# Graph layers on one Trainium2 core: softmax masks made in the logits, other node passes, no assertions, and a leak contraction in halves over four column strips

## The chip, the cores and the metric

The kernel runs on one core of one Trainium2 chip. The metric is device time in microseconds (us) of one execution. The core's engines are TensorE (PE in the profile; PEld is its weight load), VectorE (DVE), ScalarE (ACT), GpSimd (POOL) and SyncE (SP), which issues DMAs. ACT issues DMAs too, and so does POOL.

## What is computed

50000 nodes with 64 channels and 50000 edges, sorted by destination node `dst`. Four layers follow each other, and each one normalises x per node first (mean and variance over the 64 channels, then relu):

```python
h = relu(layernorm(x)); x = x + gated_conv(h, edges)      # layer 0
h = relu(layernorm(x)); x = x + edge_mlp_sum(h, edges)    # layer 1
h = relu(layernorm(x)); x = x + gatv2_twice(h, edges)     # layer 2, 5 heads, two rounds
h = relu(layernorm(x)); x = x + degree_conv(h, edges)     # layer 3, batch norm at the end

# one round of layer 2, with one self loop for each node
e = leaky_relu(xl[src] + xr[dst], 0.2)                    # 5 heads of 64 channels
alpha = einsum('ehc,hc->eh', e, att)                      # the logits
a = exp(alpha - segment_max(alpha, dst)[dst])
a = a / segment_sum(a, dst)[dst]
out = segment_sum(a * xl[src], dst).mean(heads) + bias
```

## The kernel before

The work is written out by hand for each engine, with semaphores; nothing is scheduled by a tool. `build` runs the stages one after the other, with a barrier between them (the class `Phase`). Nodes and edges are cut into 392 tiles of 128. `acc`, a buffer of 128 partitions x 27117 words, holds x or the sums.

`node_pass(layer)`, once ahead of each layer, goes over 28 groups of 14 tiles, four groups deep. DVE sums each node's channels (L595) and scales the sum to the mean (L599), POOL subtracts the mean from x (`centre`, L635), ACT squares the whole group (L660), DVE adds the squares up (L604), ACT takes the root (L665), DVE inverts it (L609) and makes h (L617, one instruction of two SBUF inputs and 896 elements). SP stores h twice, and in layer 2 x as well.

`attention_logits(g)`, for the two rounds g = 0 and 1, goes over 98 blocks of 512 edges. For each block POOL gathers the source rows by indirect DMA, and SP loads the rest. PE, in this order, transposes block n (`turn`), multiplies block n-1 by the weights (`project_whole`, L1531), takes the logits of block n-2 out of the leaky parts (`contract`) and does the last two products of block n-1 (`project_halves`, L1538). ACT makes the five leaky parts (L1572, L1577) and then issues the stores of the logits of block n-2 to `al_d` (L1563). DVE copies the transposed block (L1597), takes the logits out of PSUM (L1590) and makes the one-hot rows of a later block (L873). SP also stores the transposed block to `hsT_d` (L1491), out of a ring of two buffers: DVE's copy of block n waits for the store of block n-2.

`contract` writes one PSUM bank `alp` by strips: the output partitions fall into four strips of 32, and matmuls with 32 columns of weights on different strips run beside each other. The leaky parts q = 0, 1, 2 go to strips 0, 1, 2, the linear part (q = 5, in two matmuls of 256) goes to strip 3, and q = 4 and q = 3 are then added on strips 0 and 2. Every matmul of float32 stands in the trace as two instructions.

Ahead of its blocks each edge stage has a short loop, `fetch_rest` on POOL, `mask_rest` on DVE and `store_rest` on SP, and behind each edge stage stands `extra_pass`. Both treat the few edge tiles whose nodes lie outside the usual window, four in a turn and three turns in this run. Each turn reads four or eight tile numbers into registers, each with a check of its bounds at run time.

`softmax_stats(g)` lays the logits out as 125 rows (5 heads x 25 parts) of 2048 edges. SP loads 15 pieces of `dst_d` (own, previous and next destination) and 12 of `al_d`. DVE then makes masks out of the destinations, adds the two halves of each logit, and runs a segmented maximum and a segmented sum, each by a scan forwards and one backwards, an exchange of the rows' ends with PE, and both scans again with the carry (`both_ways`). At the end PE transposes the weights and DVE copies them out (L1755). POOL does nothing there.

## Time and profile before

| | us |
|---|---|
| median of 3 runs | 6159.76 (6159.35 to 6167.94) |
| the profiled execution | 6169.8, with a span of 6167.9 from the first instruction to the last |

| engine | busy, share of the span |
|---|---|
| PE | 4289.0 us, 70% |
| PEld | 2998.7 us, 49% |
| DVE | 3432.2 us, 56% |
| ACT | 3017.0 us, 49% |
| POOL | 3410.8 us, 55% |

The shares are averages over stages that follow each other and have different limits. So a change in one stage is read from that stage: from the rows of its timeline, and from the busy time in a window of it. Lines such as L1519 are lines of the kernel. What stands in brackets behind a row is the time for which the engine had been idle before it, and what ended that.

### The profile page before, as it was taken

The page shows a single profiled execution, that of the slowest core. Times are in us where ns is not written, and L with a number is a line of the kernel's source. Part 1 is how long each engine was busy: PE and PEld are TensorE (multiplying, and loading weights), DVE is VectorE, ACT ScalarE, POOL GpSimd, SP SyncE. Part 2 cuts the span into 40 slices and gives each one's busy share as a digit, 9 for nine tenths or more (in the row PEclk, how much of TensorE's full clock was granted, in tenths as well). Part 3 has the DMA queues.
Part 4 walks back from the last instruction along what each step waited for, and adds up shares of the span by engine and source line. Part 5 has one row for each costly group of instructions (what it writes and reads, how often), then busy time and mean ns, then how long its engine had stood idle before and what let it go on. Part 6 is the DMA issues. An engine that isn't in the chain of part 4 may idle for free. (4 is left out here: it accounts for less than half of the span.)

```text
span 6167.9 us, 123234 instructions
## 1 busy us (share of the span) xinstructions
PE 4289.0 (70%) x30675; PEld 2998.7 (49%) x30675; DVE 3432.2 (56%) x7378; ACT 3017.0 (49%) x6612; POOL 3410.8 (55%) x3519
## 2 busy tenths in 40 slices
PE   0089991499951999970995559999439877045564
PEld 0067771377740666640773236666237644035552
DVE  3834447677776222228888942222388688932256
ACT  0279992356631444430882224444138622755547
POOL 0866652566634544520886864454038699767720
PEclk9999995799975999985998989999769899567775
DMA  7566664565647444430333544444213333632224
GB/s 188 169 149 149 149 137 124 131 128 127 127 114 213 112 108 109 110 98 16 83 84 97 128 105 108 109 110 108 72 29 83 71 84 77 141 66 53 53 60 131
DMA packets 1392338, 664.98 MB, mean 108 GB/s; under 512 B 834785, under 2 KB 1339789, under 8 KB 1390450
## 3 DMA queue, kind: packets, MB, share of 16 engines
q1 hardware_dynamic: 1308640, 587.39, 38.1%
q0 software_dynamic: 64256, 65.93, 6.0%
q10 hardware_dynamic: 19320, 10.38, 0.7%
q14 instruction: 88, 0.72, 0.0%
q8 instruction: 34, 0.56, 0.0%
HBM read 393.69 MB, written 269.08 MB: 107 GB/s over the span
## 5 line engine op out<-in xcount | busy, mean ns | idle before, releaser
L849 POOL DMA_INDIRECT z_e<-h_d,src_i x784 | 770.3, 983 | 413.1 <-PE zTp_e L888 221.8
L1597 DVE COPY zT_l<-zTp_l 128x512 f32<-128x512 f32 x196 | 135.6, 692 | 1065.8 <-PE alp_l L1519 779.5
L1572 ACT ACTIVATE leak_l<-tp_l,bcat 128x512 f32<-128x512 f32 x588 | 403.7, 687 | 453.8 <-PE tp_l L1531 452.6
L734 ACT ACTIVATE hot_e<-iota_n,rel 128x256 f32<-128x256 f32 x1176 | 500.9, 501 | 232.3 <-PE part_e L747 226.3
L764 DVE TENSOR_TENSOR acc<-acc,part_e 128x128 f32 x1176 | 335.3, 285 | 472.1 <-PE part_e L747 343.0
L849 POOL DMA_INDIRECT z_l<-g_d,src_i x392 | 370.9, 946 | 350.0 <-PE zTp_l L888 255.4
L849 POOL DMA_INDIRECT z_l<-h_d,src_i x392 | 370.9, 946 | 349.9 <-PE zTp_l L888 254.9
L747 PE MATMUL part_e<-z_e,hot_e 128*128 128x128 f32 x1568 | 282.9, 355 | 383.1 <-DVE acc L1355 187.0
L1577 ACT ACTIVATE leak_l<-tp_l,bcat 128x256 f32<-128x256 f32 x784 | 307.7, 475 | 429.9 <-PE tp_l L1538 429.9
L884 PE MATMUL zTp_e<-ident,z_e 128*128 128x128 f32 x784 | 172.9, 303 | 468.7 <-DMA z_e<-rest_d 468.7
L747 PEld LDWEIGHTS part_e<-z_e,hot_e 128*128 128x128 f32 x1568 | 260.8, 260 | 405.3 <-DVE acc L1355 187.3
L734 ACT ACTIVATE hot_m<-iota_n,rel 128x256 f32<-128x256 f32 x784 | 334.3, 496 | 235.1 <-PEq L85 132.8
L1328 POOL DMA_INDIRECT z_e<-h_d,src_i x392 | 370.2, 944 | 139.9 <-issue 89.9
L635 POOL TENSOR_TENSOR xc<-acc,mean 128x896 f32<-128x896 f32 x112 | 189.0, 1688 | 453.4 <-DVE mean L599 453.0
L747 PEld LDWEIGHTS part_m<-m_m,hot_m 128*128 128x128 f32 x3136 | 365.4, 192 | 88.0 <-DVE acc L764 80.6
L747 PE MATMUL part_m<-m_m,hot_m 128*128 128x128 f32 x3136 | 402.6, 282 | 2.4 <-DVE acc L764 1.1
L747 PE MATMUL part_e<-m_e,hot_e 128*128 128x128 f32 x3136 | 386.4, 276 | 6.7 <-ACT hot_e L738 5.6
L747 PEld LDWEIGHTS part_e<-m_e,hot_e 128*128 128x128 f32 x3136 | 371.6, 192 | 16.1 <-issue 7.8
L1519 PE MATMUL alp_l<-leak_l,acat 128*32 128x512 f32 x1960 | 375.7, 600 | 3.3 <-ACT leak_l L1577 3.3
L1531 PE MATMUL tp_l<-zT_l,wcat 128*128 128x256 f32 x1176 | 371.2, 397 | 0.0
L1531 PE MATMUL tp_l<-zT_l,wswap_l 128*128 128x256 f32 x1176 | 350.2, 379 | 0.0
L884 PEld LDWEIGHTS zTp_e<-ident,z_e 128*128 128x128 f32 x784 | 79.0, 141 | 552.9 <-issue 541.3
(345 smaller groups left out, 11370.7 us busy)
## 6 DMA issues: line engine op xcount, KB each, us to landing
near_e<-near_d SPq DMA_DIRECT2D x784, 64.0 KB
near_l<-near_d SPq DMA_DIRECT2D x784, 64.0 KB
h_d<-h SPq DMA_DIRECT2D x84, 448.0 KB
near_d<-h SPq DMA_DIRECT2D x84, 448.0 KB
m_d<-m_m SPq DMA_DIRECT2D x196, 138.0 KB
relb_e<-rel_d SPq DMA_DIRECT2D x196, 128.0 KB
z_e<-rest_d SPq DMA_DIRECT2D x196, 128.0 KB
relb_l<-rel_d SPq DMA_DIRECT2D x196, 128.0 KB
```

Of the source, the lines that this page charges most:

```text
L635: nc.gpsimd.tensor_tensor(xc[g % DEEP][:, :, :], acc3[:, tiles(g), :], bc(mean[g % DEEP]), ALU.subtract).then_inc(n_cent, 1)
L734: ins = self.nc.scalar.activation(self.hots[k][:, t, :], self.S["iota_n"][:, :], ACT.Abs, scale=-1.0, bias=self.S["rel"][:, ds(n * BLK + t ...
L747: mm = self.nc.tensor.matmul(self.parts[t // 2][:, t % 2, w, :], self.hots[k][:, t, w * P:(w + 1) * P], m[:, t, :], start=True, stop=True)
L764: ins = self.nc.vector.tensor_tensor(x, x, part[:, t % 2, :, 0:x.shape[2]], ALU.add)
L849: self.nc.gpsimd.indirect_dma_start(out=self.z[n % RINGS][:, t, SIDES[t % 2]], out_offset=None, in_=self.table[:, :], in_offset=bass.Indir ...
L884: self.nc.tensor.matmul(zTp[:, t * P:(t + 1) * P], self.z[k][:, t, :], ident[:, :], start=(t == 0), stop=False, is_transpose=True, skip_gr ...
L1328: nc.gpsimd.indirect_dma_start(out=z[k][:, t, 0:C], out_offset=None, in_=S["h_d"][:, :], in_offset=bass.IndirectOffsetOnAxis(ap=S["src_i"] ...
L1519: mm = nc.tensor.matmul(alp[at:at + STRIP, :], acat[:, q, :], leak[k][:, q, :], start=(q in (0, 1, 2)), stop=(q not in (0, 2)))
L1531: mm = nc.tensor.matmul(by_side(tp[q])[:, side], left[:, q, :], by_side(zT[k])[:, side], start=True, stop=True)
L1572: nc.scalar.activation(leak[u % 2][:, q, :], tp[q][:, :], ACT.Relu, bias=bcat[:, 0, q:q + 1], scale=1.0 - SLOPE).then_inc(leak_ready, 1)
L1577: nc.scalar.activation(by_side(leak[u % 2][:, 3 + q, :])[:, side], tp[3 + side][:, q * 2 * P:(q + 1) * 2 * P].rearrange("p (r e) -> p r e" ...
L1597: nc.vector.tensor_copy(zT[k][:, :], zTp[k][:, :]).then_inc(zT_ready, 1)
```

## The change

1. **Logits, `contract`.** q = 4 is added on strips 0 and 1, one half of the block's 512 columns on each, and q = 3 on strips 2 and 3. A second weight tile `alate` gives q = 3 its place in strip 3. The logits of a block leave in six stores in place of four.
2. **Masks.** A class `Scan` owns the views of `acc` from ahead of the logits on. The 15 loads of `dst_d` are issued by ACT at the start of the logits. DVE makes the masks, and two new scans over them (`pf`, `pb`: is there no border between here and the row's end), between its first six blocks.
3. **Early loads.** Behind its last loads for the blocks, and ahead of the last three stores to `hsT_d`, SP issues 20 loads of the first 22 of 25 parts of each row. `softmax_stats` loads the other 3 parts by 20 small DMAs, ten on SP and ten on ACT.
4. **Softmax.** No reductions over the masks; in place of the second scans, one instruction each combines the held mask, the carry and the first scan. ACT takes over one mask and the copies of `als`, POOL takes over three operations on the self-loop side, and the division by 5 goes into another instruction.
5. **Node passes of layers 1 and 2.** The mean is subtracted on DVE, POOL does nothing, and ACT squares tile by tile, 14 instructions per group, each with the sum as its accumulator output. DVE's sum of the squares goes away.
6. **Assertions.** The loads of tile numbers in `mask_rest`, `store_rest` and `extra_pass` are made with no check of their bounds.

```diff
-STRIP_OF = (0, 1, 2, 2, 0, 3)
-STRIP_ORDER = (0, 1, 2, 5, 4, 3)
-STRIP_ROWS = ((0, 0, 4), (1, 4, 2), (2, 6, 4), (3, 10, 10))
+EARLY = 22
+AL_ROWS = ((0, 1, 4, 5, 6), (8, 9, 2, 3, 7))
+HALVES = (slice(0, BLK * P // 2), slice(BLK * P // 2, BLK * P))
+STRIP_ROWS = ((0, 0, 0, 2, ALL), (0, 2, 2, 2, HALVES[0]), (1, 0, 4, 2, ALL), (1, 2, 2, 2, HALVES[1]), (2, 0, 6, 4, ALL), (3, 0, 10, 10, ALL))
...
                 for g in range(G + 3):
                     if g < G:
                         add_up(g)
-                    if 2 <= g < G + 2:
+                    if 2 <= g < G + 2 and not SUMS_ON_ACT:
                         spread(g - 2)
+                    if g >= 3 and SUMS_ON_ACT:
+                        normalise(g - 3)
                     if g < G:
                         take_mean(g)
+                        if SUMS_ON_ACT:
+                            centre(g)
...
+                        for b in range(GRP):
+                            ins = nc.scalar.activation(sq[k][:, b, :], xc[k][:, b, :], ACT.Square, accum_out=var[k][:, b:b + 1])
+                        ins.then_inc(n_var, 1)
...
-                                                            min_val=0, max_val=TILES - 1)[1]
+                                                            min_val=0, max_val=TILES - 1,
+                                                                   skip_runtime_bounds_check_because="setup makes these numbers out of clamped tiles")[1]
...
+    def masks(self, dve, chain, step):
+        if step == 1:
+            dve.wait_ge(self.s_dst, 15 * 16)
+            chain(nc.vector.tensor_copy(self.tot, self.own.bitcast(I32)))
+            chain(nc.vector.tensor_copy(self.fwd, self.prev.bitcast(I32)))
+            chain(nc.vector.tensor_copy(self.bwd, self.nxt.bitcast(I32)))
+        if step == 2:
+            chain(nc.vector.tensor_tensor(self.prev, self.fwd, self.tot, ALU.is_equal))
+            chain(nc.vector.tensor_tensor(self.nxt, self.bwd, self.tot, ALU.is_equal))
+        if step == 3:
+            chain(nc.vector.tensor_scalar(self.pen_f, self.prev, 1.0, BIG, ALU.subtract, ALU.mult))
+            chain(nc.vector.tensor_scalar(self.pen_b, self.nxt, 1.0, BIG, ALU.subtract, ALU.mult))
+        if step == 4:
+            chain(nc.vector.tensor_tensor_scan(self.pf, self.prev, self.prev, 1.0, ALU.mult, ALU.min))
+        if step == 5:
+            chain(nc.vector.tensor_tensor_scan(self.pb[:, rev], self.nxt[:, rev], self.nxt[:, rev], 1.0, ALU.mult, ALU.min))
+            chain(nc.vector.tensor_scalar(self.own, self.pf, 1.0, BIG, ALU.subtract, ALU.mult))
...
+                def early():
+                    sp.wait_ge(scans.s_masked, 1)
+                    for k in range(2):
+                        sp.wait_ge(al_out[k], 96 * (EARLY * SCAN_W // (BLK * P) // 2))
+                    for part, pair in enumerate(((scans.lg, scans.ls), (scans.mx, scans.tot))):
+                        for side in range(2):
+                            scans.load_logits(sp, S["al_d"], pair[side], part, side, 0, EARLY, scans.s_early)
...
-                    for q in STRIP_ORDER:
-                        at = STRIP_OF[q] * STRIP
...
+                    for x, left, q, cols in ((0, acat[:, 4, :], 4, HALVES[0]), (1, acat[:, 4, :], 4, HALVES[1]),
+                                             (2, acat[:, 3, :], 3, HALVES[0]), (3, alate[:, :], 3, HALVES[1])):
+                        mm = nc.tensor.matmul(alp[strip(x), cols], left, leak[k][:, q, cols], start=False, stop=True, skip_group_check=True)
...
+                nc.gpsimd.tensor_tensor(ls, ls, tot, ALU.add).then_inc(self_sum, 1)
+
+                pool.wait_ge(s_a, 2)
+                nc.gpsimd.tensor_tensor(kept, prev, ls, ALU.mult).then_inc(self_kept, 1)
+                pool.wait_ge(self_kept, 1)
+                nc.gpsimd.tensor_tensor(kept, ls, kept, ALU.subtract).then_inc(self_kept, 1)
...
+                scans.load_logits(act, al_d, mx, 1, 0, EARLY, T, e_in)
+                scans.load_logits(act, al_d, tot, 1, 1, EARLY, T, x_in)
+                nc.scalar.activation(ppb, pb, ACT.Copy, scale=BIG, bias=-BIG).then_inc(s_pen, 1)
...
-                    chain(scan(fwd, gain_f, data, carry[:, 0:1], op0, op1))
-                    chain(scan(bwd[:, rev], gain_b[:, rev], data[:, rev], carry[:, 1:2], op0, op1))
+                    dve.wait_ge(s_pen, 1)
+                    chain(stt(out=fwd, in0=held_f, scalar=carry[:, 0:1], in1=fwd, op0=op0, op1=op1))
+                    chain(stt(out=bwd, in0=held_b, scalar=carry[:, 1:2], in1=bwd, op0=op0, op1=op1))
...
-                chain(ts(tot, tot, 1.0 / H, None, ALU.mult))
-                chain(tt(lg, lg, tot, ALU.mult))
-                chain(tt(ls, ls, tot, ALU.mult))
-                chain(ts(own, prev, -1.0, 1.0, ALU.mult, ALU.add))
-                chain(tt(ls, ls, own, ALU.mult))
+                chain(stt(out=lg, in0=lg, scalar=1.0 / H, in1=tot, op0=ALU.mult, op1=ALU.mult))
+                chain(stt(out=ls, in0=kept, scalar=1.0 / H, in1=tot, op0=ALU.mult, op1=ALU.mult))
```

On PE, the first `contract` of round 0, before (L1519 are the leaky parts, L1517 the linear one, L1538 the next product):

```order
L1519 MATMUL alp_l0<-leak_l0_0,acat0 32x512 x3
L1517 MATMUL alp_l0<-zT_l0_0,acat0 32x2x128
L1517 MATMUL alp_l0<-zT_l0_0,aswap_l0_0 32x2x128
L1519 MATMUL alp_l0<-leak_l0_0,acat0 32x512 x2
L1538 MATMUL tp_l0_3<-zT_l0_1,wcat0 128x256
```

and now:

```order
L1594 MATMUL alp_l0<-leak_l0_0,acat0 32x512 x3
L1596 MATMUL alp_l0<-zT_l0_0,acat0 32x2x128
L1596 MATMUL alp_l0<-zT_l0_0,aswap_l0_0 32x2x128
L1599 MATMUL alp_l0<-leak_l0_0,acat0 32x256 x3
L1599 MATMUL alp_l0<-leak_l0_0,alate_l0_0 32x256
```

The two matmuls of 512 columns at the end of the contraction have become four of 256.

On DVE, in the middle of the node pass of layer 1, before:

```order
564 L595 TENSOR_REDUCE mean_0<-acc 128x14
565 L604 TENSOR_REDUCE var_2<-sq_2 128x14
566 L599 TENSOR_SCALAR mean_0<-mean_0 128x14
567 L609 RECIPROCAL rstd_1<-rstd_1 128x14
568 L617 SCALAR_TENSOR_TENSOR h_1<-xc_1,rstd_1 128x896
```

and now:

```order
504 L599 TENSOR_REDUCE mean_0<-acc 128x14
505 L613 RECIPROCAL rstd_1<-rstd_1 128x14
506 L621 SCALAR_TENSOR_TENSOR h_1<-xc_1,rstd_1 128x896
507 L603 TENSOR_SCALAR mean_0<-mean_0 128x14
508 L627 TENSOR_TENSOR xc_0<-acc,mean_0 128x896
```

The sum of the squares has left DVE, and the subtraction of the mean has come to it.

On DVE, the first blocks of the logits of round 0, where the masks (the rows on `acc`) now stand:

```order
1224 L1681 COPY zT_l_0<-zTp_l_0 128x512
1225 L1499 CAST acc<-acc 125x2048
1226 L1500 CAST acc<-acc 125x2048
1227 L1501 CAST acc<-acc 125x2048
1228 L894 TENSOR_SCALAR hotT_l_0<-relb_l_2,iota_p 128x512 x2
1229 L1681 COPY zT_l_1<-zTp_l_1 128x512
1230 L1503 TENSOR_TENSOR acc<-acc 125x2048
1231 L1504 TENSOR_TENSOR acc<-acc 125x2048
1232 L894 TENSOR_SCALAR hotT_l_1<-relb_l_3,iota_p 128x512 x2
```

Before, the copy of a block was followed at once by the one-hot rows (L873) of the next.

## Rows read from the trace of the kernel before

**Rows 1.** Busy time by window: node passes of layers 1 and 2, then logits.

```profile
core 0: us, PE busy (x) PEld busy (x) DVE busy (x) ACT busy (x) POOL busy (x), PEclk, DMA share, GB/s
985.00:1090.00 105.00, 0.00 (x0) 0.00 (x0) 102.95 (x110) 27.43 (x45) 36.97 (x22) 0.50 0.66 192
1820.00:1920.00 100.00, 0.00 (x0) 0.00 (x0) 97.95 (x106) 26.39 (x42) 35.43 (x21) 0.50 0.91 288
...
2300.00:2400.00 100.00, 100.00 (x715) 60.52 (x705) 27.81 (x52) 47.42 (x92) 49.81 (x54) 1.00 0.46 110
```

**Rows 2.** Timeline (start, length, engine and line, operation): PE, a contraction and the next.

```profile
2307.03 0.63 PE L1519 MATMUL alp_l<-leak_l,acat 128*32 128x512 f32 x3
...
2307.92 1.03 PE L1519 MATMUL alp_l<-leak_l,acat 128*32 128x512 f32 x4
...
2308.88 0.48 PE L1538 MATMUL tp_l<-zT_l,wcat 64*128 64x256 f32 x1
...
2314.65 0.63 PE L1519 MATMUL alp_l<-leak_l,acat 128*32 128x512 f32 x3
```

**Rows 3.** Timeline: ACT's last stores of a block's logits, its next leak.

```profile
2311.15 1.20 ACTq L1563 DMA_DIRECT2D al_d<-logit_l  x3
...
2313.03 0.69 ACT L1572 ACTIVATE leak_l<-tp_l,bcat 128x512 f32<-128x512 f32 x1 [1.41 <-PE tp_l L1531]
```

**Rows 4.** Timeline: SP's loads of destinations at the softmax's start.

```profile
2742.42 5.94 SPq L1648 DMA_DIRECT2D acc<-dst_d  x15
```

**Rows 5.** DMA queues, packets, MB, share of 16 engines, from 2742 to 2800 us.

```profile
q1 hardware_dynamic: 1050, 7.17, 35.7%
```

**Rows 6.** Timeline: DVE in the softmax of both rounds.

```profile
2790.52 2.29 DVE L1691 TENSOR_TENSOR acc<-acc 125x2048 f32<-125x2048 f32 x1 [51.70 <-DMA acc<-al_d]
...
2795.17 1.23 DVE L1694 CAST acc<-acc 125x2048 f32<-125x2048 int32 x1
...
2847.18 2.29 DVE L1705 TENSOR_REDUCE flag_s<-acc 125x1 f32<-125x2048 f32 x1 [3.83 <-ACT acc L1683]
...
2866.10 4.48 DVE L1728 TENSOR_TENSOR_SCAN acc<-acc,carry_s 125x2048 f32<-125x2048 f32 x1
...
2909.24 3.52 DVE L1755 COPY als<-pt_s 128x125 f32<-128x125 f32 x16
...
4438.37 2.29 DVE L1691 TENSOR_TENSOR acc<-acc 125x2048 f32<-125x2048 f32 x1 [57.71 <-DMA acc<-al_d]
```

**Rows 7.** Timeline: POOL and DVE in layer 1's node pass, and after POOL's last.

```profile
1008.76 1.69 POOL L635 TENSOR_TENSOR xc<-acc,mean 128x896 f32<-128x896 f32 x1 [3.10 <-DVE mean L599]
...
1008.93 2.47 DVE L617 SCALAR_TENSOR_TENSOR h<-xc,rstd 128x896 f32<-128x896 f32 x1
...
1011.32 1.07 DVE L595 TENSOR_REDUCE mean<-acc 128x14 f32<-128x896 f32 x1
1012.32 1.07 DVE L604 TENSOR_REDUCE var<-sq 128x14 f32<-128x896 f32 x1
...
1013.71 2.46 DVE L617 SCALAR_TENSOR_TENSOR h<-xc,rstd 128x896 f32<-128x896 f32 x1
...
1098.74 1.09 DVE L617 SCALAR_TENSOR_TENSOR h<-xc,rstd 128x896 f32<-128x896 f32 x1
```

**Rows 8.** Timeline: ACT's small instructions in layer 3, and its accumulator reads.

```profile
5301.31 3.43 ACT L673 ACTIVATE hd<-h,dsc 128x64 f32<-128x64 f32 x14
...
6035.09 0.19 ACT L2270 ACTIVATION_READ_ACCUMULATOR y_f<-acc,col_f 128x1 f32 x1
6035.18 0.71 ACT L2270 ACTIVATE y_f<-acc,col_f 128x512 f32<-128x512 f32 x1
```

**Rows 9.** Timeline: DVE's idle time behind loads of tile numbers.

```profile
926.20 0.72 DVE L764 TENSOR_TENSOR acc<-acc,part_e 128x128 f32 x2 [0.33 <-issue]
...
957.59 0.63 DVE L1430 TENSOR_TENSOR at_r<-dstf,extra_lo 128x1 f32 x4 [3.66 <-issue]
...
1970.76 0.15 DVE L817 COPY left_l<-dst_i 128x1 int32 x1 [2.12 <-issue]
```

180 lines of the change are left out of this document (112 added, 68 removed).

## The prediction

> **What bounds the kernel now.** No engine bounds the whole: the stages do, each by something else. I read the busy time by window first, to find what is full in each stage that the change touches, and then the timeline there. The profiled execution took 6169.8 us (span 6167.9), 10 us over the median of the runs; the sum is made against the former and then lowered by 10.
>
> In the logits PE is busy for the whole of the window, at full clock, while DVE is busy for 28%, ACT for 47%, POOL for 50% and DMA for 46% [rows 1]. From one contraction to the next are 2314.65 - 2307.03 = 7.62 us, of which the contraction holds 1.85: 0.89 to the start of its last group, 0.96 from there to the next product [rows 2]. So what PE saves per block is saved 98 times in each round.
>
> In the softmax only DVE works, and first it stands idle for 51.7 us in round 0 and 57.7 in round 1 until its inputs have come [rows 6].
>
> In the node passes of layers 1 and 2 DVE is busy for 98% [rows 1]. A group takes 1013.71 - 1008.93 = 4.78 us, and of that 2.47 go to an instruction that takes 1.09 once POOL has stopped [rows 7]: DVE waits there for POOL's subtraction, which started 0.17 earlier. In layer 2 DMA is at 0.91 too.
>
> **Contraction in halves.** The first round of strips stays. In the last group two strips take 512 columns each, and now four take 256. The first group shows four strips side by side in 0.89 us for 512 columns each, so I take it that four halves too run side by side: 0.43 us instead of 0.86. Gain 0.43 x 98 x 2 = **84 us**. What is late next? POOL needs 5.0 us of the new 7.19 per block, DVE 2.1, so neither. ACT issues six stores instead of four, at 0.40 each; they end at 2312.35 now and the next leak starts at 2313.03 [rows 3], so they end about at the same point as that start, and PE reads this leak only in the next block but one. Bounds of this term: 0 (two halves follow each other) to 90.
>
> **Masks and loads in the logits.** DVE gets three casts, two comparisons, two masks, two scans and one more mask in five pieces, 3.7 to 5.7 us each from 1.23 for a one-input operation, 2.29 for two inputs and 4.48 for a scan [rows 6]. In a block of 7.2 us it has 5.1 free, and PE needs the copy of a block about 2 us after it can be made. Only the first piece stands where the blocks still ramp up; I charge 3 us. ACT's 15 loads are 3 MB, issued at 0.40 each [rows 4] while the short loop gathers rows; 7.17 MB took 48.1 us in the softmax [rows 5, 6], so 3 MB take 20, beside three turns of about 10 us. They cost the small gathers some latency: 4 us (0 to 12). For two rounds **+14 us**.
>
> **Early loads.** 20 x 22 x 8 KB = 3.6 MB, at that rate 24 us. They go into SP's queue right behind the store of block 94. The store of block 95 is queued behind them, and DVE's copy of block 97 waits for it: three blocks, 21.5 us, later. So it comes some 5 us late, PE waits for that copy and may take up its last block at a lower clock. I charge **8 us** a round (0 to 15). What is gained is DVE's wait: from the last logit (2790.52 - 51.70 = 2738.8) to SP's first load at 2742.4 [rows 4, 6] stay 3.6 us, and then ten small loads on each of two queues need about 4 us to issue and 2 to land. So DVE starts 10 us after the last logit in place of 51.7 and 57.7: 41.7 + 47.7.
>
> **Softmax chain**, per round, by DVE instructions that go [rows 6]: one addition and the masks 2.3 + 3 x 1.25 + 2 x 2.3 + 2 x 1.25 = 13.2; four reductions 9.2; four scans of 4.5 become one pass each of two inputs, 2.3, which is 8.8; of the 3.83 us of waiting for both exponentials 0.2 stay, 3.6; at the end two one-input passes and one two-input pass, 4.8; of the 3.5 for the copies of als, ACT's run beside the others and 0.5 stays, 3.0. Sum 42.6. Against it stand POOL's three passes. Scaled from 1.69 for 896 elements [rows 7] each takes 3.9 us for 2048, and DVE's two-input instruction in rows 7 waited for the whole of POOL's. If all three are waited for, they cost 11.6; if the second and third fall beside the 5 us exchange with PE, less; no row shows a scan against POOL. I take 8 (0 to 11.6), near the upper end because of rows 7. Net 34.6.
>
> The Trainium skill (SBUF — State Buffer, Who interferes with whom) says that a DVE instruction with two SBUF inputs contends with a GpSimd instruction that reads SBUF, and that the loser fully blocks. The trace agrees for L617. By that rule alone the charge would be 11.6 and the sum 7 us smaller; by a cost that only POOL bears it would be 16 larger.
>
> Softmax in all: 41.7 + 47.7 - 2 x 8 + 2 x 34.6 = **143 us**.
>
> **Node passes.** DVE's group becomes a sum, a reciprocal, h in 1.09, the mean, and the subtraction, about 1.09 as well: some 3.7 us. ACT's becomes 14 squares with accumulator and a root. Fourteen instructions of 64 elements with a scale from memory started 0.24 apart (3.43 less the last one's end, over 13), and a read of the accumulator puts 0.09 between its start and the next instruction's [rows 8]: 14 x 0.33 + 0.2 = 4.8 us, no gain. The square has no scale from memory and should be cheaper, with 0.17 at the lowest: 3.9. I take 4.1, since the squares are plain. Layer 1 gains 0.7 x 28 = 19. In layer 2 DMA at 0.91 lets 4.78 fall to 4.4 at most [rows 1]: 8. Together **27 us** (from a loss of 5 to 37).
>
> **Assertions.** DVE is idle for 3.66 us behind two checked loads and 2.12 behind one, so a checked load costs up to 1.54; an unchecked one, 0.33 or less [rows 9]. So a check costs some 1.2. In `extra_pass` both of DVE's loads lie on the path of each turn: 5 passes x 3 turns x 2.4 = 36. In the short loops one: 4 x 3 x 1.2 = 14. **50 us** (25 to 65). SP's loads run beside DVE's.
>
> **Sum.** 84 + 143 - 14 + 27 + 50 = 290 us. 6169.8 - 290 = 5880, and 10 less for the median: **5870 us**.
>
> **Rivals.**
> 1. The halves do not run side by side: the sums on strips 0 and 1 read the same weights and the same leaky part. If two follow two, the last group keeps 0.86, and the 84 us are gone: 5954. If all four follow each other it takes 1.72 and PE gets slower by 168: 6122. Against it: the first group's four strips, two of which read the same buffer too.
> 2. ACT bounds the node passes. If a square takes its whole 0.33 us and the read its whole 0.19, a group takes 14 x 0.52 + 0.3 = 7.6 us, 2.8 over now, 157 us for both passes: 5870 + 184 = 6054. Against it: the rows show both overlapped.
> 3. The wait moves: the small loads queue behind each other or behind the early ones, and half of the 89 us of DVE's wait stay: 5915.
> 4. Slower than before: the six stores per block. ACT's own work is 47% of 7.62, 3.6 us per block, and if its sequencer issues a store only between computations, a block takes 3.6 + 6s. That exceeds PE's 7.19 from s = 0.6 on, and eats up all other gains (206 us, 1.05 per block over 7.62) from s = 0.85. At s = 1.0 a block takes 9.6 us: 5964 + 1.98 x 196 = 6352. The rows have s = 0.40, beside running computations.
> 5. The change does less than it says: were only the contraction and the early start to work, with chain, node passes and assertions without effect, 84 + 89 - 30 = 143 us would remain: 6017.
>
> **How the numbers follow.** The forecast with its small variations has 0.66, by itself 5810 to 5930; rival 1 0.10 (mostly its milder form), rival 2 0.08, rival 3 0.09, rival 4 0.02, rival 5 0.05. Below the forecast stand: no stall at the logits' end (16), no wait for POOL (16), node passes and assertions at their ends (10 and 15), dst loads for nothing (8). The range 5800 to 5960 takes these in, rival 3 and the milder rival 1, and leaves out the rest, some 0.18. A measurement of this kernel can tell about 0.2% (12 us) from no change. Faster: all but rival 4 and a residue, 0.96; the same 0.01; slower 0.03.
>
> **What would show it.** Right: contractions 7.2 us apart, with 0.5 us in the last group; DVE's first instruction of the softmax some 10 us after the last logit, and copies of al ending 85 to 90 us later; groups of 4.1 us in layer 1 and 4.4 in layer 2; idle time of 1.3 us at the start of a turn of `extra_pass`. Wrong: a wait of PE for a leak in the middle of the logits; more than 10 us of PE idle ahead of its last block; accumulator reads 0.5 us apart; DVE instructions of 2048 elements lengthened by more than 12 us in all, beside POOL.

## The result, and the profile after

The changed kernel takes 5905.49 us in the median of four runs (5902.51 to 5907.38), beside 6160.15 us for the kernel before in the same session: a ratio of 0.958, with a 95% interval of 0.9568 to 0.9593. The forecast was 5870 us, the range 5800 to 5960. The profiled execution took 5907.4 us with a span of 5905.6, so between the two traces lie 262 us; the forecast had 290.

**Contraction.** Timeline of PE in the logits of the first round (start, length, engine and line, operation, count), against [rows 2]:

```profile
2625.26 0.63 PE L1594 MATMUL alp_l<-leak_l,acat 128*32 128x512 f32 x3
...
2626.14 0.39 PE L1599 MATMUL alp_l<-leak_l,acat 128*32 128x256 f32 x3
...
2626.69 0.48 PE L1618 MATMUL tp_l<-zT_l,wcat 64*128 64x256 f32 x1
...
2632.46 0.63 PE L1594 MATMUL alp_l<-leak_l,acat 128*32 128x512 f32 x3
```

The next contraction follows after 7.20 us, not 7.62, and the last group holds 0.55 us, not 0.96. The forecast said 7.2 and 0.5.

**Far rows.** Ahead of the blocks, three turns gather 12 tiles of far rows. DVE waits for a gather in each of four masks of a turn. Here are its timeline in the first and second turn and, in the DMA view from 1898 to 1938 us (bytes of a tile, then median us from issue to landing), what was in flight:

```profile
1907.61 0.26 DVE L845 TENSOR_SCALAR hotT_l<-hotT_l,far_l 128x64 f32<-128x64 f32 x1 [6.93 <-DMA hotT_l<-h_d,left_l]
...
1912.17 0.15 DVE L838 COPY left_l<-dst_i 128x1 int32 x1 [1.03 <-issue]
...
1920.51 0.25 DVE L845 TENSOR_SCALAR hotT_l<-hotT_l,far_l 128x64 f32<-128x64 f32 x1 [7.39 <-DMA hotT_l<-h_d,left_l]
1924.09 0.26 DVE L845 TENSOR_SCALAR hotT_l<-hotT_l,far_l 128x64 f32<-128x64 f32 x1 [3.33 <-DMA hotT_l<-h_d,left_l]
```

```profile
q10 hardware_dynamic: 450, 3.07, 20.0%
q1 hardware_dynamic: 1904, 0.71, 7.8%
q0 software_dynamic: 412, 0.43, 5.0%
...
acc<-dst_d ACTq DMA_DIRECT2D x15, 200.0 KB
...
hotT_l<-h_d,left_l POOLq DMA_INDIRECT x12, 5.5
```

The second turn starts 1.03 us behind the first one's end, where it was 2.16: the assertion is gone. But the gathers come late. The new 3.07 MB lie on ACT's queue (q10) beside them. From the first turn's start to the last mask the trace before has 28.02 us in round 0 and 27.67 in round 1, the trace after 37.84 and 39.71. For the kernel before, the same waits read:

```profile
1954.38 0.25 DVE L824 TENSOR_SCALAR hotT_l<-hotT_l,far_l 128x64 f32<-128x64 f32 x1 [2.73 <-DMA hotT_l<-h_d,left_l]
1955.80 0.27 DVE L824 TENSOR_SCALAR hotT_l<-hotT_l,far_l 128x64 f32<-128x64 f32 x1 [1.17 <-DMA hotT_l<-h_d,left_l]
```

Turn by turn round 0 takes 12.4, 17.5 and 8.0 us, where it took 10.0, 10.1 and 7.9. In the first turn only the landing of the gathers is late. In the second POOL also asks for them late: it gathers into the buffers out of which SP stores the first turn's rows to `rest_d`, and waits for these stores. Here are POOL's first operation of the second turn (a small addition ahead of its first gather), now and before, and the DMA view from 1907 to 1912 us, with the four stores of the first turn:

```profile
1914.81 0.19 POOL L829 TENSOR_TENSOR spare_l<-iota_p 128x1 f32<-128x1 f32 x1 [8.79 <-DMA rest_d<-hotT_l]
```

```profile
1961.14 0.19 POOL L808 TENSOR_TENSOR spare_l<-iota_p 128x1 f32<-128x1 f32 x1 [4.34 <-DVE far_l L818]
```

```profile
rest_d<-hotT_l SPq DMA_DIRECT2D x4, 32.0 KB, 8.9
```

The stores of the kernel before's first turn land after 1.5 us.

**The logits' end and the start of the softmax.** Timelines of SP's queue, DVE and POOL, against [rows 6]:

```profile
2629.42 7.77 SPq L1491 DMA_DIRECT2D acc<-al_d  x20
...
2637.23 1.21 SPq L1560 DMA_DIRECT2D hsT_d<-zT_l  x2
```

```profile
2677.14 2.29 DVE L1793 TENSOR_TENSOR acc<-acc 125x2048 f32<-125x2048 f32 x1 [10.85 <-DMA acc<-al_d]
2679.46 4.42 DVE L1798 TENSOR_TENSOR_SCAN acc<-acc 125x2048 f32<-125x2048 f32 x1
2683.92 8.53 DVE L1799 TENSOR_TENSOR_SCAN acc<-acc 125x2048 f32<-125x2048 f32 x1
...
2726.85 2.47 DVE L1808 TENSOR_TENSOR_SCAN acc<-row_s 1x125 f32<-1x125 f32 x1
```

```profile
2681.22 6.95 POOL L1765 TENSOR_TENSOR acc<-acc 125x2048 f32<-125x2048 f32 x1 [60.90 <-DMA acc<-al_d]
2713.70 6.78 POOL L1768 TENSOR_TENSOR acc<-acc 125x2048 f32<-125x2048 f32 x1 [25.53 <-ACT acc L1780]
2720.56 8.49 POOL L1770 TENSOR_TENSOR acc<-acc 125x2048 f32<-125x2048 f32 x1
```

DVE starts 10.85 us after the last logit (forecast 10) where it was 51.70. DVE copies block 95 by 2634.8, SP issues its store at 2637.23, behind the 20 loads, and it lands behind their 3.6 MB, 17.6 us later. Block 97's copy waits for that landing:

```profile
2654.79 0.69 DVE L1681 COPY zT_l<-zTp_l 128x512 f32<-128x512 f32 x1 [12.06 <-DMA hsT_d<-zT_l]
```

PE waits for that copy, and takes up its last block with products of 1.22 us, where the same two took 0.70 in the block before; its granted clock is 0.50 (1.2 GHz) from 2655 to 2658 us, behind 6.12 us in which it did nothing, and was 1.00 (2.4 GHz) from 2640 to 2648:

```profile
2655.54 1.22 PE L1611 MATMUL tp_l<-zT_l,wcat 128*128 128x256 f32 x2 [6.12 <-DVE zT_l L1681]
```

Beside POOL the reverse scan takes 8.53 us, not 4.42. POOL's first operation starts at 2681.22, inside the forward scan that ends at 2683.88, and ends at 2688.17: 4.29 us after the scan's end. The reverse scan, issued at 2683.92, ends at 2692.45, which is 4.28 us after POOL's end. Both figures are near the 4.42 us of the undisturbed scan and the 3.9 that I had expected of POOL, so I read them as each engine's own work, none of it beside the other's. DVE copies al by 2765.0, 87.9 us after its first operation.

**Node pass of layer 1 and turns of an extra pass.** DVE, against [rows 7] and [rows 9], then the busy time by window in the passes of layers 1 and 2, against [rows 1]:

```profile
1004.09 1.08 DVE L599 TENSOR_REDUCE mean<-acc 128x14 f32<-128x896 f32 x1
1005.09 0.23 DVE L613 RECIPROCAL rstd<-rstd 128x14 f32<-128x14 f32 x1
1005.42 1.09 DVE L621 SCALAR_TENSOR_TENSOR h<-xc,rstd 128x896 f32<-128x896 f32 x1
...
1006.64 1.09 DVE L627 TENSOR_TENSOR xc<-acc,mean 128x896 f32<-128x896 f32 x1
1007.64 1.08 DVE L599 TENSOR_REDUCE mean<-acc 128x14 f32<-128x896 f32 x1
```

```profile
949.43 0.63 DVE L1454 TENSOR_TENSOR at_r<-dstf,extra_lo 128x1 f32 x4 [1.44 <-issue]
```

```profile
core 0: us, PE busy (x) PEld busy (x) DVE busy (x) ACT busy (x) POOL busy (x), PEclk, DMA share, GB/s
1000.00:1060.00 60.00, 0.00 (x0) 0.00 (x0) 57.64 (x86) 60.00 (x494) 0.00 (x0) 0.50 0.89 259
1800.00:1860.00 60.00, 0.00 (x0) 0.00 (x0) 46.83 (x70) 50.91 (x410) 0.00 (x0) 0.50 1.00 303
```

A group of layer 1 takes 3.55 us (forecast 4.1, before 4.78). In layer 2 the first twelve groups take 3.55 too; from then on DVE waits for stores of h out of the ring, most groups take 4.4 to 4.7, and the DMA share is 1.00.

**Where the 262 us are.** Each number is a time in the traces from DVE's first instruction of a stage to its first of the next. In the logits that is now the fill of the new weight tile, 1.7 us ahead of the first turn; from the first turn on, the logits take 1534.4 us, 41.7 less, and the pass ahead of them is then 4.6 shorter, not 6.3.

| stage | before | after | less |
|---|---|---|---|
| edges of layer 0 (with the wait ahead of its extra pass) | 659.8 | 651.5 | 8.3 |
| node pass, layer 1 | 141.2 | 113.8 | 27.4 |
| edges of layer 1 | 665.2 | 660.8 | 4.4 |
| node pass, layer 2, up to the logits | 147.0 | 140.7 | 6.3 |
| logits to the last logit, both rounds | 1576.2 | 1537.8 | 38.4 |
| last logit to the first softmax operation, both | 109.4 | 21.9 | 87.5 |
| softmax, both | 251.8 | 187.6 | 64.2 |
| five extra passes | 121.0 | 99.8 | 21.2 |
| all else | | | 4.6 |

### The profile page after: what moved, and what is told of

The parts are those of the page before. It is cut to its first block and busy times, and to the rows that moved or that the text cites. A ratio compares the mean times of both kernels' runs of the same rounds, so it can differ in the third digit from the quotient of the medians.

```text
span 5905.6 us, 126888 instructions
## 1 busy us (share of the span) xinstructions
PE 4208.6 (71%) x31459; PEld 3024.1 (51%) x31459; DVE 3357.9 (57%) x7332; ACT 3145.2 (53%) x8158; POOL 3384.5 (57%) x3469
## 5 line engine op out<-in xcount | busy, mean ns | idle before, releaser
L1681 DVE COPY zT_l<-zTp_l 128x512 f32<-128x512 f32 x196 | 135.5, 691 | 959.5 <-PE alp_l L1599 692.8
L870 POOL DMA_INDIRECT z_l<-h_d,src_i x392 | 384.6, 981 | 300.1 <-PE zTp_l L909 203.5
L870 POOL DMA_INDIRECT z_l<-g_d,src_i x392 | 384.8, 982 | 299.2 <-PE zTp_l L909 202.3
L767 PEld LDWEIGHTS part_m<-m_m,hot_m 128*128 128x128 f32 x3136 | 365.2, 192 | 87.9 <-DVE acc L784 80.6
L905 PE MATMUL zTp_l<-ident,z_l 128*128 128x128 f32 x784 | 173.6, 304 | 251.7 <-DMA z_l<-rest_d 248.3
L2175 DVE TENSOR_TENSOR prod_a<-xl_a,wself_a 128x640 f32<-128x640 f32 x392 | 303.8, 814 | 56.1 <-PE xl_a L2062 56.0
```

What stands on the lines that cost most here:

```text
L767: mm = self.nc.tensor.matmul(self.parts[t // 2][:, t % 2, w, :], self.hots[k][:, t, w * P:(w + 1) * P], m[:, t, :], start=True, stop=True)
L870: self.nc.gpsimd.indirect_dma_start(out=self.z[n % RINGS][:, t, SIDES[t % 2]], out_offset=None, in_=self.table[:, :], in_offset=bass.Indir ...
L905: self.nc.tensor.matmul(zTp[:, t * P:(t + 1) * P], self.z[k][:, t, :], ident[:, :], start=(t == 0), stop=False, is_transpose=True, skip_gr ...
L1681: nc.vector.tensor_copy(zT[k][:, :], zTp[k][:, :]).then_inc(zT_ready, 1)
L2175: nc.vector.tensor_tensor(prod[k][:, 2 * q:2 * q + 2, :].rearrange("p t (h c) -> p t h c", h=H), xl[slot(u, q)][:, :, 0:HC].rearrange("p t ...
```

## Experiments

Runs of one group ran on one chip. In groups one and two the kernel before took 6497.7 and 6500.0 us, in group three 6166.2. Where the groups differ is told at the end; a run is compared with the changed kernel on its own kind of chip (groups one and two were two chips of one kind), and small effects are read from the length of their stage, since a ratio's interval is some 8 us to either side.

### Group one

**The contraction alone**, in the kernel before:

```diff
-                    for q in STRIP_ORDER:
...
+                    for x, left, q, cols in ((0, acat[:, 4, :], 4, HALVES[0]), (1, acat[:, 4, :], 4, HALVES[1]),
+                                             (2, acat[:, 3, :], 3, HALVES[0]), (3, alate[:, :], 3, HALVES[1])):
...
-                    for strip, at, rows in STRIP_ROWS:
+                    for strip, row, at, rows, cols in STRIP_ROWS:
```

> The kernel before with only the contraction of the change: the fourth and fifth leak in halves over the four column strips, the extra left-hand tile, and six stores of logits a block instead of four. Theory: the contraction is the bound of the logits in both rounds, its period goes from 7.62 to 7.19 us and nothing else moves, so 196 blocks save 84 us: 6160 becomes about 6076 us, and each round's logits take 746 instead of 788 us from the first mask turn to the last logit. Rival: the two more stores a block on ScalarE's queue or their landing hold the logit tiles back and eat half of it; each round's logits would take 767 us and the kernel 6118 us.

Measured: 6441.4 us, ratio 0.9914 (0.9899 to 0.9929), 56 us less, 46 to 66 by the interval. The gain lies between the theory's 84 and the rival's 42. The logits take 770.3 and 769.0 us from the first turn to the last logit, near the rival's 767, but not for the rival's reason: on this chip the first logit comes 32 to 34 us after DVE's first comparison for the blocks (the first of `hotT`), where the kernel before has 21 to 22 on the first chip. In the blocks of round 0 PE's recorded waits sum to 4 us, most of them for ACT's leaky parts; the changed kernel on the first chip has 0.2 us of them. Median distance of two logits: 7.24 and 7.26 us. From the first logit to the last are 704.4 and 701.1 us, against 732.9 in both rounds of the kernel before on the first chip. So the halves do run beside each other, and no wait of DVE for the stores of the logits stands among its waits; but of 84 us this run shows at most 66. There is no trace of the kernel before on this chip, so the whole gain is only known here from the times.

**Loads of node numbers late**, in the changed kernel:

```diff
+                act.wait_ge(z_used, 1)
                 scans.load_nodes(act, S["dst_d"])
...
-                        scans.masks(dve, chain, n)
+                        scans.masks(dve, chain, n - 3)
```

> The changed kernel with the 15 loads of node numbers issued on ScalarE's queue only when TensorE has used the first block of rows, and the five mask steps on VectorE three blocks later (ten blocks of the logits are written out ahead of the loop, not six). Theory: in the changed kernel these loads run beside the three turns that gather the far rows and lengthen them from 28.0 to 37.8 us a round, though a turn has lost its assertion; moved behind, the turns take about 25.5 us, the logits of each round are 12 us shorter, and the kernel goes from 5905 to about 5881 us. Rival: the loads take the same DMA time from the first blocks' row loads instead, TensorE waits there as long, and the kernel stays at 5905 us. Second rival: the turns are long for another reason (their own gathers or the code), and stay at 37.8 us.

Measured: 6285.0 us; the changed kernel takes 6275.9 on such a chip (group two). The turns take 25.83 and 25.72 us, as the theory said; so the loads had lengthened them. But the first logit comes 48.7 and 50.5 us behind DVE's first comparison, where the changed kernel has 32.3 and 31.6 on such a chip, and the stage up to the softmax's first operation is 0 and 8 us longer. DVE's timeline shows for what it waits there:

```profile
2194.94 0.88 DVE L894 TENSOR_SCALAR hotT_l<-relb_l,iota_p 128x512 f32<-128x512 bf16 x2 [17.66 <-DMA relb_l<-rel_d]
2206.60 0.69 DVE L1682 COPY zT_l<-zTp_l 128x512 f32<-128x512 f32 x1 [10.78 <-DMA hsT_d<-zT_l]
```

The first rival is right: the wait went to the next in line for the DMA engines.

**One store first**, in the changed kernel:

```diff
-    if between is not None:
-        between()
     for n in range(NB - lag, NB):
         then(n, n)
+        if n == NB - lag and between is not None:
+            between()
```

> The changed kernel with the 20 early loads of logits issued behind the first of the last three stores of rows, not ahead of it. Theory: VectorE's 12.06 us idle at the last but one block is the wait for that one store, which lies on SyncE's queue behind 20 loads; it goes, the last logit comes 6 us earlier in each round, and the early loads still land before the late ones: 5905 becomes about 5893 us, with VectorE's first softmax operation still 11 us behind the last logit. Rival: the early loads land so much later that softmax waits for them: the 6 us come back there (17 us behind the last logit) and the kernel stays at 5905 us.

Measured: 6265.7 us, 10 less than the changed kernel in group two. The last five logits come 7.10, 7.30, 7.09, 5.08 and 7.42 us apart, 34.0 us in all; in the changed kernel on such a chip it is 7.09, 7.31, 13.37, 7.42 and 4.21, 39.4. The stall at block 97 has gone, and part of it came back at the last one, where DVE now waits for stores of logits:

```profile
2915.82 0.75 DVE L1674 TENSOR_SCALAR logit_l<-alp_l,lin_b 128x512 f32<-128x512 f32 x1 [6.67 <-DMA al_d<-logit_l]
2927.70 2.29 DVE L1793 TENSOR_TENSOR acc<-acc 125x2048 f32<-125x2048 f32 x1 [11.13 <-DMA acc<-al_d]
```

Softmax starts 11.1 us behind the last logit, as before. The order in SP's queue was the larger half of the stall; the 3.6 MB in flight are the rest.

**GpSimd's three operations on VectorE**, in the changed kernel:

```diff
-            @block.gpsimd
-            def _(pool):
...
+                chain(tt(ls, ls, tot, ALU.add))
...
+                chain(tt(kept, prev, ls, ALU.mult))
+                chain(tt(kept, ls, kept, ALU.subtract))
```

> The changed kernel with GpSimd's three operations of the softmax (the sum of the two self logits and two for the kept part, each 125x2048) given to VectorE. Theory: in the changed kernel GpSimd working beside VectorE lengthens two reverse scans from 4.42 to 8.53 us and one scan of the row from 0.41 to 2.47 us, 10.3 us a round; on VectorE the three cost 3 x 2.3 = 6.9 us, so each chain gets 3.4 us shorter, 90 becomes 86.7 us, and the kernel goes from 5905 to about 5899 us. Rival: the scans are long for what they read or write now, not for GpSimd: they stay at 8.53 us, the three operations come on top, and the kernel goes to 5919 us.

Measured: 6265.6 us, 10 less. The softmax takes 90.43 us in the first round and 90.40 in the second, against 93.77 and 93.78 in the first trace of the changed kernel and 93.35 and 93.76 in its second: 2.9 to 3.4 less, where the theory had 3.4. The scans are short again:

```profile
2930.93 4.42 DVE L1787 TENSOR_TENSOR_SCAN acc<-acc 125x2048 f32<-125x2048 f32 x1
2935.39 4.42 DVE L1788 TENSOR_TENSOR_SCAN acc<-acc 125x2048 f32<-125x2048 f32 x1
```

So 6 to 7 of the 10 us are shown to be of this edit; the rest is within what the times vary.

### Group two

**The changed kernel again**, unedited:

> The changed kernel once more, so that the next three have it on their own chip. Theory and rival alike: ratio to the kernel before of 0.958 where the edge stages take what they took in the first pair of traces, nearer to 0.964 on a chip where those take longer; the three turns that gather the far rows take 37.8 us in the logits of the first round.

Measured: 6275.9 us, ratio 0.9655 (0.9642 to 0.9668). Turns 38.44 and 37.36 us, first logit 32.3 and 31.6 us behind DVE's first comparison, 719.1 and 717.1 us from the first logit to the last (first chip 700.4 and 702.1).

**Loads of node numbers spread**, three for each of five blocks:

```diff
+                def loads(n, u, i):
+                    body(n, u, i)
+                    if isinstance(n, int) and 2 <= n < 7:
+                        scans.load_nodes(act, S["dst_d"], n - 2)
...
-                        scans.masks(dve, chain, n)
+                        scans.masks(dve, chain, n - 7)
```

> The changed kernel with the 15 loads of node numbers issued by ScalarE three at a time behind its work on blocks 2 to 6, and the mask steps on VectorE at blocks 8 to 12 (14 blocks written out ahead of the loop). Theory: the loads cost time only where all 3 MB of them lie on the DMA engines at once, first beside the gathers' turns (37.8 us instead of 25.8), then beside the first blocks; three a block fit into what the steady blocks leave free, so the turns take 25.8 us, the first logit comes no later than in the changed kernel behind the turns, and each round gains 12 us: 24 us less than the changed kernel on this chip. Rival: the 3 MB cost their 12 us wherever they are put; the blocks beside them get longer by as much, and the kernel takes what the changed one takes.

Measured: 6271.6 us, 4 less. Turns 25.87 and 25.83 us, 12 less, and the first logit hardly later (32.7 us in both rounds); but from the first logit to the last are 730.1 and 726.2 us, 11 and 9 more. Up to the softmax's first operation a round gains 1.6 us. DVE waits at block 7 for a store and then for the last of the loads, issued 10 us before:

```profile
2233.27 0.69 DVE L1686 COPY zT_l<-zTp_l 128x512 f32<-128x512 f32 x1 [8.59 <-DMA hsT_d<-zT_l]
...
2239.41 1.23 DVE L1500 CAST acc<-acc 125x2048 f32<-125x2048 int32 x1 [4.78 <-DMA acc<-dst_d]
```

On this chip the rival is right: 3 MB cost about the same beside the turns and beside the first blocks. On the first kind of chip, where PE hardly waits in the blocks, there is no such run.

**Early loads spread**, five behind each of SP's last four blocks of loads, with `EARLY` at 21:

```diff
+    for j in range(ends):
+        n = NB - ends + j
+        first(n, n)
+        then(n - lag, n - lag)
+        between(j)
```

> The changed kernel with the 20 early loads of logits issued five at a time behind SyncE's row loads and stores of the last four blocks it loads for (which are written out behind the loop), and 21 of 25 segments early instead of 22. Theory: the wait of VectorE for one store behind the lump of 20 loads (12.06 us idle) and the wait of the last logit for its stores (found in the run with one store ahead: 7.42 instead of 4.22 us) both come of the lump; spread, the last five logits come 7.1, 7.3, 7.1, 4.6 and 4.2 us apart, 8 us a round sooner, less 1 us for the larger late part: about 14 us less than the changed kernel. Rival: SyncE falls behind with its row loads, TensorE waits for them in the last blocks, and nothing is gained.

Measured: 6265.9 us, 10 less. The last five logits are 7.09, 7.31, 7.09, 4.62 and 4.22 us apart in both rounds: no stall is left, and 9.1 and 7.5 us are gained there (39.4 and 37.8 to 30.3). DVE starts 11.6 and 12.6 us behind the last logit, 0.4 and 1.9 more. In the second round the turns (40.31 us for 37.36) and the other blocks were slower by nearly as much, so that the stage is only 0.6 us shorter; the whole shows less than the end of the logits does, and the same edit comes again below.

**The node pass of layer 0 as well**:

```diff
-    SUMS_ON_ACT = layer in (1, 2)
+    SUMS_ON_ACT = layer in (0, 1, 2)
```

> The changed kernel with the node pass of layer 0 done as that of layers 1 and 2 is: VectorE subtracts the mean, ScalarE squares and sums; GpSimd keeps its one addition a group (2.92 us). Theory: what made VectorE's operations long in these passes is GpSimd at work beside them, and one operation of GpSimd a group is enough for it; VectorE has 3.55 us of work alone and about 1.4 us more beside the addition, so a group takes 4.9 us against 4.79 and layer 0 gains nothing (0 to 5 us slower). Rival: it was the number of steps on VectorE; the group takes 3.6 us as in layer 1 and the kernel gets 30 us faster than the changed one.

Measured: 6301.0 us, 25 more. The pass takes 160.9 us, not 141.1, which is 20 of the 25. DVE's and POOL's timelines:

```profile
180.29 1.09 DVE L621 SCALAR_TENSOR_TENSOR h<-xc,rstd 128x896 f32<-128x896 f32 x1
181.30 0.17 DVE L603 TENSOR_SCALAR mean<-mean 128x14 f32<-128x14 f32 x1
181.50 2.98 DVE L627 TENSOR_TENSOR xc<-acc,mean 128x896 f32<-128x896 f32 x1
...
185.76 1.09 DVE L621 SCALAR_TENSOR_TENSOR h<-xc,rstd 128x896 f32<-128x896 f32 x1
```

```profile
181.47 2.07 POOL L656 TENSOR_TENSOR acc<-acc,h 128x896 f32<-128x896 f32 x1 [3.40 <-DVE h L621]
```

POOL starts its addition 0.03 us ahead of DVE's subtraction, and that takes 2.98 us instead of 1.09: about the whole addition (2.07) and then itself. A group takes 5.47 us; I expected 4.9. The direction of the theory holds, and the rival (the number of DVE's steps) falls; the price was too small: I took 1.4 us from the old pass, where POOL's operation had begun earlier, and it is 1.9.

### Group three

**A third of the bytes**: the masks from the own node numbers, shifted by one:

```diff
-        for off, dst in ((1, self.own), (0, self.prev), (2, self.nxt)):
+        for off, dst, cols in ((1, self.own, slice(0, W)), (0, self.prev, slice(0, 2)), (2, self.nxt, slice(W - 2, W))):
...
-            chain(nc.vector.tensor_tensor(self.prev, self.fwd, self.tot, ALU.is_equal))
+            chain(nc.vector.tensor_tensor(self.prev[:, 1:], self.tot[:, 0:last], self.tot[:, 1:], ALU.is_equal))
```

> The changed kernel with one third of the bytes in the loads of node numbers: only the own numbers come in five loads of 25 rows of 8 KB, and for the previous and the next numbers just the one column at a row's end that the own ones don't hold (ten loads of 8 bytes a row); VectorE makes the two masks out of the own numbers shifted by one. They stay where the change put them. Theory: the turns that gather the far rows are longer in the changed kernel by the bytes that share the DMA engines with the gathers, 12 us for 3.1 MB; with 1.0 MB they take 29 to 31 us instead of 37.8 to 39.7, a round gains 7 to 9 us, and two casts less on VectorE 1 us more: 16 to 20 us less than the changed kernel. Rival: it is the fifteen loads' count or ScalarE's queue, not the bytes; the turns stay at 37 us or more.

Measured: 5887.3 us, ratio 0.9549 (0.9536 to 0.9562), against 0.958 for the changed kernel: 20 us less. The turns take 29.68 and 30.02 us. There are still fifteen loads on the same queue at the same place; only the bytes went. The gathers' rows in the DMA view, from 1896 to 1928 us:

```profile
q10 hardware_dynamic: 450, 1.03, 9.3%
...
hotT_l<-h_d,left_l POOLq DMA_INDIRECT x12, 2.5
```

Their median landing goes from 5.5 to 2.5 us. Turn by turn round 0 takes 12.5, 9.3 and 7.8 us, beside 12.4, 17.5 and 8.0. So the whole gain is in the second turn, and there it was the bytes: the first turn's stores land after 3.7 us, not 8.9. The first turn is as long as before this edit, its gathers land after 6.0 us in both kernels, and two thirds of the bytes less change nothing in it. Whether it is long for the megabyte that is left, or for the number of loads, isn't shown.

**The three gains together** (smaller loads, early loads spread, the softmax without GpSimd):

> The changed kernel with what the runs so far gave, put together: the smaller loads of node numbers, the early loads of logits five at a time behind the last four blocks' loads, and GpSimd's three softmax operations on VectorE. Theory: the three lie in different stages (far rows' turns, end of the logits, softmax) and add up: 8, 6 and 3.4 us a round, together about 35 us less than the changed kernel, a ratio to the kernel before of about 0.952 on a chip like the first and 0.960 on one like that of the other runs. Rival: what one gives another takes (the early loads wait for the masks, the first blocks for their rows), and it gains 20 us or less.

Measured: 5865.3 us (5862.3 to 5869.5), ratio 0.9512 (0.9499 to 0.9525). This beats the changed kernel, whose interval ends at 0.9568, by 0.7%, 42 us. By stage, against the changed kernel's first trace: turns 29.5 and 30.6 us (8.3 and 9.1 less), first logit to last 692.8 us in both rounds (7.6 and 9.3 less), softmax 90.4 (3.3 less in each), start of the softmax 12.3 and 11.8 us behind the last logit (1.5 and 0.7 more). The last copies are no longer held up:

```profile
2642.68 0.69 DVE L1687 COPY zT_l<-zTp_l 128x512 f32<-128x512 f32 x1 [5.74 <-PE alp_l L1605]
...
2652.13 0.75 DVE L1680 TENSOR_SCALAR logit_l<-alp_l,lin_b 128x512 f32<-128x512 f32 x1 [3.47 <-PE alp_l L1605]
...
2665.19 2.29 DVE L1788 TENSOR_TENSOR acc<-acc 125x2048 f32<-125x2048 f32 x1 [12.31 <-DMA acc<-al_d]
```

**Old node passes** in the changed kernel:

```diff
-    SUMS_ON_ACT = layer in (1, 2)
+    SUMS_ON_ACT = False
```

> The changed kernel with the node passes of layers 1 and 2 as they were: GpSimd subtracts the mean, VectorE sums the squares. Theory: layer 1's pass goes from 113.8 back to 141.2 us up to the first edge operation; layer 2's is held by its three stores and gives back 6 us at the most; together 33 us more than the changed kernel. Rival: layer 2's pass has no other bound either and gives back 27 us too; 54 us more.

Measured: 5933.6 us, ratio 0.9627 (0.9612 to 0.9642), 28 us more than the changed kernel by the medians and 22 between the traces, where 33 was expected. Layer 1's pass takes 141.24 us, 27.4 more; layer 2's takes 144.6, 3.9 more. The edge stage of layer 1 takes 657.3 us, where the three traces of this kind of chip with the new passes and no assertions have 659.9 to 660.8. So the change of the passes is worth 31 us by the two stages and 22 to 28 by the whole, and DMA does bound layer 2's: most of what it could gain goes into waits for stores.

**Assertions back** in the changed kernel:

```diff
-                                                             skip_runtime_bounds_check_because="setup makes these numbers out of clamped tiles")[1]
+                                                             )[1]
```

> The changed kernel with the assertions on the tile numbers put back in the turns of the extra passes and of the far rows. Theory: a turn of an extra pass takes 2.2 us more (fifteen turns, 33 us) and a turn of the far rows 0.8 us more in layers 0 and 1 (5 us), none in the logits, where the gathers end later anyway: 38 us more than the changed kernel. Rival: the turns in the logits get their 1.2 us each too, and the kernel takes 50 us more, as I forecast.

Measured: 5948.5 us, ratio 0.9646 (0.9631 to 0.9661), 41 us more by the ratio, 43 by the medians and 44 between the two traces. A turn of an extra pass idles for 3.66 us again. The far rows' turns in the logits take 36.00 and 39.62 us, no more than in the changed kernel: there the gathers end later than the check.

## Why the forecast held, and where it was 28 us too high

The mechanisms of the forecast were right, but for one term: the loads of node numbers, where a part of it was missing. The time is in the range; the sum is 28 us too high. Term by term, with what the traces and runs give on the first kind of chip. The rows come from different runs, so that they add up to the 262 only within some 5 us:

| term | forecast | found | from |
|---|---|---|---|
| contraction | 84 | 80 | first to last logit 732.94, and 692.77 with no stall: 40.2 a round |
| DVE's mask steps | -6 | about 0, not told apart | in the same 692.77 |
| stall at the logits' end | -16 | -17 | 700.39 and 702.07 against 692.77 |
| loads of node numbers | -8 | -22 | turns 28.02 to 37.84 and 27.67 to 39.71 |
| early loads | 89 | 87.5 | stage table |
| softmax chain | 69 | 64 | stage table |
| node passes | 27 | 28 (31 by the stages) | run with the old passes |
| assertions | 50 | 42 | run with the assertions back |
| sum | 290 | 262 | between the traces 262 |

**Loads of node numbers** is the step that failed: "They cost the small gathers some latency: 4 us (0 to 12)". I had the bytes and the time they take (20 us), and treated the wait of a gather as a small addition to it. But a turn stands on two landings, one behind the other: that of its gathers, and that of the last turn's stores, which must have left the buffers. With the loads beside them the first turn's gathers land after 6.0 us and its stores after 8.9, not 1.5. Net it was 10 and 12 us a round; against the 25.8 us that three turns without assertion need when the loads are gone, it was 12 and 14, at or over the upper end of the range. Two runs that put the loads elsewhere, on the other kind of chip, gave the time back elsewhere, and the run with fewer bytes gained 18 us in the turns.

**Assertions**: a check in an extra pass's turn costs 1.1 us (idle time from 3.66 to 1.44 for two), not 1.2: 33 us for fifteen turns in place of 36 (22 in the table's row of extra passes, 11 ahead of DVE's first instruction in each, in the rows above it). In the turns of the far rows of layers 0 and 1 it is 1.0 to 1.2 us for each of the two checks between three turns (28.3 to 25.9 and 27.5 to 25.5, up to the last mask), and 0.7 and 1.1 for the one ahead of the first turn: 6 us. In the logits only the check ahead of the first turn counts (idle time 2.50 in the run with the assertions back, 1.39 without: 2 us for both rounds); between the turns the gathers were late anyway. That makes 41 us. That the same turns carry the assertion's gain and the loads' cost was missed: where two terms fall on one stretch, they don't add.

**Softmax chain**: I charged 8 us for POOL's three operations, scaled from 1.69 us for 896 elements to 3.9 for 2048. One takes 4.29 beyond the scan that it waits for, two are waited for by a scan in full, and the third in part: (8.53 - 4.42) x 2 + 2.47 - 0.41 = 10.3 us. The Trainium skill (SBUF — State Buffer, Who interferes with whom) says that a DVE instruction with two SBUF inputs contends with a GpSimd instruction that reads SBUF, and that the one that loses the shared ports is blocked for the whole of the other. The scan's row and the run without POOL agree with it (8.53 to 4.42 us), and so does the run with layer 0's pass (2.98 for 1.09). By that rule my charge would have been 11.6, as the prediction says; of the third operation DVE met only the end, with a short scan that took 2.47 us and not 0.41.

**Contraction**: 0.41 us a block instead of 0.43. **Early loads**: DVE started 10.85 and 11.03 us behind the last logit instead of 10. **Stall**: 7.6 and 9.3 us for 8.

**Node passes**: 3.55 us a group for 4.1. The squares with their reads of the accumulator stand 0.24 us apart, pair by pair, so 14 take 3.4 us; I had put a group at 4.1 (a square's read starts 0.15 us behind it in ACT's timeline, and the next square 0.09 behind the read; the forecast's lowest for the square, 0.17, stands in no row). ACT is busy for 60.00 of 60 us in the window above and DVE for 57.64, so both are full. Layer 1 gave 27.4 for 19, and layer 2 gave 3.9 by the run, not 8. That their sum came so near is in part luck: layer 1 was put 8 us too low and layer 2 some 4 us too high.

**The rivals.** The halves run beside each other (0.55 us for the last group), so the first falls. The second falls by its price: ACT is full, but at 3.55 us a group and not at 7.6. The third, that the wait moves, falls for the start of the softmax (10.85 us) but describes well what the loads of node numbers did. The fourth falls: six stores a block, and PE's recorded waits in the blocks of round 0 sum to 0.2 us on the first chip, none of them for ACT. The fifth falls, as chain, node passes and assertions were each worth what they were said to be within a sixth.

## What to carry to other kernels

A load that is moved to where "nothing else needs the DMA engines" must be weighed against every wait for a landing in that stretch, however small the transfers: here 3 MB beside gathers and stores of 32 KB cost 12 us and more a round, and moving them only chose another victim on the chips where that was run. Count the landings that stand one behind the other, stores that free a buffer among them. Fewer bytes helped at once: three loads of nearly the same numbers became one and a shifted reading of it. On an issue queue, a lump of loads belongs behind the one store that somebody waits for, or in pieces between the steady loads. And GpSimd is no free helper for a chain of two-input VectorE operations: give it what falls beside something else, or do it on VectorE.

## What the runs showed of the hardware that I had not expected

- **DMA half idle, and yet full for the one who waits.** During the far rows' turns the mean share of the DMA engines is 0.16 before, 0.25 with a third of the bytes and 0.32 in the changed kernel, and the gathers' median landing goes from 2.5 us with a third of the bytes to 5.5. From 1912 to 1928 us, while the stores that take 8.9 us are on their way, it is 0.35. Which of the engines or steps is full there isn't shown. Busy time by window, of the kernel before, of the changed one and of the one with a third of the bytes, in this order:

```profile
1950.00:1978.00 28.00, 0.00 (x0) 0.00 (x0) 5.75 (x35) 0.00 (x0) 14.79 (x25) 0.50 0.16 34
```

```profile
1900.00:1937.00 37.00, 0.00 (x0) 0.00 (x0) 5.37 (x34) 0.00 (x0) 14.80 (x25) 0.50 0.32 107
```

```profile
1898.00:1927.00 29.00, 0.00 (x0) 0.00 (x0) 5.30 (x33) 0.00 (x0) 14.84 (x25) 0.50 0.25 68
```

- **Chips differ by stage.** With the same kernel, the chips of groups one and two differ from the first. The one of group two takes 778.3 us for the edges of layer 0 and 761.3 for those of layer 1, where the first takes 651.5 and 660.8, and its first logit comes 10 us later. The softmax (93.4 to 93.8 us), layer 1's node pass (113.8) and the extra passes of layers 0 and 1 (19.6 to 20.5) agree to some tenths. The long stages are those that gather rows. Each chip was used once, so whether it is the chip or the hour isn't shown. So a gain of DMA time that is measured on one chip need not hold on the other; the gains on the engines that were measured on both (softmax, node pass) did.
- **Accumulator reads are nearly free.** A square of 64 elements with its read takes 0.24 us from one to the next, no more than such an operation with a scale from memory and no read ([rows 8]: 3.43 us for 14).
